# Cross-attention on one Trainium2 core: matmuls regrouped into two-step cycles over three turning pairs of PSUM banks

## What is computed

```python
x = x + _L0_attn_ref(_layernorm(x), gamma, Wq, Wkv, Wo)
x = x + _L0_xattn_ref(_layernorm(x), ctx_2048, mask, Wq, bq, Wk, bk, Wv, bv, Wo, bo, ...)
x = x + _L0_ffn_ref(_layernorm(x), gate_w, gate_b, val_w, val_b, out_w, out_b)
# inside the cross-attention
k = proj(ctx, Wk, bk); v = proj(ctx, Wv, bv)
scores = clip(einsum('bhsd,bhtd->bhst', q, k) / sqrt(16), -50, 50)
scores = where(attend, scores, -10000); scores = clip(scores, -50, 50)
ctx = einsum('bhst,bhtd->bhsd', softmax(scores), v)
delta = ctx @ Wo.T + bo          # then a layernorm, scaled and added
```

## Time and profile before

| | before |
|---|---|
| median of 3 executions | 1391.52 us (1391.16 to 1392.73) |
| the profiled execution | 1393.63 us |
| its span, first to last instruction | 1391.8 us |
| PE busy | 1369.9 us, 98% |
| DVE busy | 996.4 us, 72% |
| ACT busy | 719.7 us, 52% |
| POOL busy | 512.0 us, 37% |
| granted TensorE clock, mean | 0.998 |

### The profile page before, as it was taken

How to read it: one execution, slowest core, us unless ns; L and a number is a source line. 1 busy time by engine, 2 the same in 40 slices (tenths; PEclk the granted TensorE clock), 3 DMA queues, 4 the chain that set the end, 5 groups by cost and what they waited for, 6 DMA issues and landing times.

```text
span 1391.8 us, 55872 instructions
## 1 busy us (share of the span) xinstructions
PE 1369.9 (98%) x25409; PEld 1171.4 (84%) x25409; DVE 996.4 (72%) x1824; ACT 719.7 (52%) x943; POOL 512.0 (37%) x491
## 2 busy tenths in 40 slices
PE   8999999999999999999999999999999999999997
PEld 6788888886888888888888888888888888888884
DVE  5688788785346867777676867677776868677766
ACT  3545454543555555555555555555554555555550
POOL 2656666551324233333323332433333242333310
PEclk9999999999999999999999999999999999999999
DMA  7010001010411211121212121121212112111100
GB/s 193 1 36 1 32 1 32 2 52 1 127 55 47 65 47 50 47 65 32 68 32 78 51 62 50 47 65 32 65 32 80 42 55 65 48 51 47 51 3 8
DMA packets 38957, 66.81 MB, mean 48 GB/s; under 512 B 3749, under 2 KB 36962, under 8 KB 38722
## 3 DMA queue, kind: packets, MB, share of 16 engines
q1 hardware_dynamic: 38722, 63.24, 15.6%
HBM read 61.40 MB, written 1.84 MB: 45 GB/s over the span
## 4 chain that ended last, share of the span: by engine, by line
PE 72%; DVE 2%; issue 0%; POOL 0%; DVEq 0%
PE proj_ps L1479 20%; PE proj_ps L1470 20%; PE score_ps L1497 15%; PE sum_ps L1522 13%; PE side_ps L1557 2%; PE side_ps L1571 1%; PE side_ps L1539 1%; PE side_ps L1564 1%; DVE amax L1357 0%; DVE hidden L1379 0%; DVE sig L1389 0%; DVE hidden L1390 0%; PE side_ps L1546 0%; DVE exps L1279 0%; DVE totals L1301 0%
## 5 line engine op out<-in xcount | busy, mean ns | idle before, releaser
L1231 ACT ACTIVATE exps<-score_ps 125x1792 f32<-125x1792 f32 x192 | 320.4, 1669 | 431.0 <-PE score_ps L1497 431.0
L1279 DVE TENSOR_SCALAR exps<-exps,top 125x896 f32<-125x896 f32 x384 | 287.9, 791 | 21.8 <-ACT exps L1231 17.5
L1497 PE MATMUL score_ps<-spread,keys 32*125 32x112 f32 x6144 | 219.0, 279 | 0.0
L1270 DVE COPY vals<-proj_ps 125x512 f32<-125x512 f32 x192 | 129.5, 687 | 116.7 <-PE proj_ps L1479 114.4
L1522 PEld LDWEIGHTS sum_ps<-exps,vals 125*32 125x32 f32 x12288 | 163.1, 110 | 47.1 <-issue 34.2
L1497 PEld LDWEIGHTS score_ps<-spread,keys 32*125 32x125 f32 x6144 | 184.8, 183 | 15.4 <-issue 0.3
L1522 PE MATMUL sum_ps<-exps,vals 125*32 125x56 f32 x12288 | 191.6, 215 | 0.0
L1159 POOL TENSOR_TENSOR low<-raw_early,high 128x500 fp32r<-128x500 f32 x64 | 84.5, 1322 | 216.8 <-PE proj_ps L1470 215.9
L1159 POOL TENSOR_TENSOR low_early<-raw_early,high_early 128x500 fp32r<-128x500 f32 x62 | 89.4, 1459 | 168.7 <-PE proj_ps L1470 168.7
L1223 ACT ACTIVATE keys<-proj_ps,b_k 128x500 f32<-128x500 f32 x192 | 129.9, 677 | 23.9 <-PE proj_ps L1470 20.4
L331 POOL TENSOR_TENSOR swapped<-swapped,sin 128x448 f32<-128x448 f32 (+1 forms) x69 | 81.0, 1175 | 85.6 <-ACT swapped L615 80.3
(11 more groups left out here) (187 smaller groups left out, 2702.7 us busy)
## 6 DMA issues: line engine op xcount, KB each, us to landing
raw_early<-in_ctxT SPq DMA_DIRECT2D x64, 500.0 KB, 4.2
raw<-in_ctxT SPq DMA_DIRECT2D x32, 500.0 KB, 3.6
w_q<-in_attn_Wq SPq DMA_DIRECT2D x4, 512.0 KB, 9.6
out<-y_out SPq DMA_DIRECT2D x16, 112.0 KB, 2.5
rows<-in_x SPq DMA_DIRECT2D x1, 1344.0 KB, 18.1
raw_early<-in_attn_Wo SPq DMA_DIRECT2D x1, 1024.0 KB, 17.5
raw_early<-in_ffn_gate_wT SPq DMA_DIRECT2D x1, 1024.0 KB, 5.3
raw_early<-in_ffn_val_wT SPq DMA_DIRECT2D x1, 1024.0 KB, 4.9
```

Of the source, the lines that this page charges most:

```text
L1231: nc.scalar.activation(exps[t % 2][:, :, :, :].rearrange("p h r n -> p r h n"), score_ps[0:TILE, :, 0:2 * QW].rearrange("p r (h n) -> p r ...
L1270: nc.vector.tensor_copy(vals[r][:, 2 * q:2 * q + 2, :, 0:HD], proj_ps[q][0:TILE, :].rearrange("p (k h d) -> p k h d", k=2, d=HD))\
L1279: nc.vector.tensor_scalar(tile, tile, LIMIT_LO, top[:, n, at:at + 1], ALU.max, ALU.min)\
L1497: ins = nc.tensor.matmul(score_ps[0:TILE, r, to:to + HE * S], keys[c % 2][32 * r:32 * r + 32, k, (at + half) * TILE:(at + half + 1) * TILE ...
```

## The change

PE's `body` now goes by chunk (`TWINS` = 6 a pair, called a cycle `m` here). With e = 2m and o = 2m + 1 it issues S(e), then A(e-2) and A(e-1) directly behind each other, then S(o), then all four pieces, K and V, of the next chunk. Four runs take the place of six, and tail steps of an odd `t` stand between K and V.

The six banks behind scores and pieces are dealt out anew. `strip_ps` (two banks) takes the second half of every step's scores. Two `pair_ps` of two banks take turns between the first half of the scores and the pieces. S(o) waits for the strip half of the exponential of e and for the copies of the values out of its other two banks; K waits for the whole exponential of e. The exponential of a step is two instructions now, over two banks each, strip half first. A third buffer `exps` lets A lag two steps.

On DVE the limits of e and o stand behind their own exponentials, and both copies of values at the end of the cycle; `divide` and `quantise_hidden` (`AHEAD`, 0 and 10) stand ahead of the limits. On SP each load also waits for the odd scores before it. On POOL the first `power` of a tail stands ahead of the low parts of cycle 1.

```diff
-GATES = (7, 8)
-AFTER = (2, 5)
+TWINS = NT // 2
+SLOTS = 3
@@
-        score_ps = ctx.enter_context(nc.psum_tensor("score_ps", [P, HR, 512], F32))
-        proj_ps = [ctx.enter_context(nc.psum_tensor(f"proj_ps{n}", [P, 512], F32)) for n in range(2)]
+        strip_ps = ctx.enter_context(nc.psum_tensor("strip_ps", [P, HR // 2, 512], F32))
+        pair_ps = [ctx.enter_context(nc.psum_tensor(f"pair_ps{n}", [P, 2, 512], F32)) for n in range(2)]
@@
+        def score_bank(t, r):
+            return pair_ps[(t // 2 + t) % 2][0:TILE, r, :] if r < HR // 2 else strip_ps[0:TILE, r - HR // 2, :]
+        def piece_bank(x, p):
+            return pair_ps[(x + 1) % 2][:, p % 2, :]
@@ SP
                         sp.wait_ge(low_ready, DC * (PC * i + c))
+                        sp.wait_ge(scores_ready, NT * i + 2 * c)
@@ POOL
                 for c in range(PC):
+                    if c == 1 and not first:
+                        power(2 * (i - 1))
@@
                     if c == 1 and not first:
-                        power(2 * (i - 1))
                         power(2 * (i - 1) + 1)
@@ ACT, exp_twin
                 if warm:
-                    act.wait_ge(probs_used, NT * i + t - 1)
-                nc.scalar.activation(exps[t % 2][:, :, :, :].rearrange("p h r n -> p r h n"),
-                                     score_ps[0:TILE, :, 0:2 * QW].rearrange("p r (h n) -> p r h n", h=2),
-                                     ACT.Exp, scale=0.25).then_inc(exps_ready, 1)
+                    act.wait_ge(probs_used, NT * i + t - SLOTS + 1)
+                for at, banks in ((HR // 2, strip_ps), (0, pair_ps[(t // 2 + t) % 2])):
+                    nc.scalar.activation(
+                        exps[t % SLOTS][:, :, at:at + HR // 2, :].rearrange("p h r n -> p r h n"),
+                        banks[0:TILE, :, 0:2 * QW].rearrange("p r (h n) -> p r h n", h=2),
+                        ACT.Exp, scale=0.25).then_inc(exps_ready, 1)
@@ PE, piece
                 elif not cold:
-                    pe.wait_ge(vals_ready, 2 * x + p - 1)
+                    pe.wait_ge(exps_ready, 2 * (2 * x - 1))
@@ PE, scores
-                if warm:
-                    pe.wait_ge(exps_ready, NT * i + t)
+                if t % 2:
+                    pe.wait_ge(exps_ready, 2 * (NT * i + t) - 1)
+                    pe.wait_ge(vals_ready, 2 * (PC * i + c) + 2)
+                elif warm:
+                    pe.wait_ge(exps_ready, 2 * (NT * i + t))
@@ PE, body
+                for m in range(TWINS):
+                    e, o = 2 * m, 2 * m + 1
+                    x, r = PC * i + m + 1, (m + 1) % 2
+                    scores(i, e, not first or e >= 1)
+                    for n in (e - 2, e - 1):
+                        if n >= 0:
+                            add_up(i, n, not first or n >= BN)
+                        elif not first:
+                            add_up(i - 1, NT + n, True)
+                    scores(i, o)
+                    if e in tail:
+                        tail[e]()
+                    if not (last and m == PC - 1):
+                        piece(x, 0, r)
+                        piece(x, 1, r)
+                    if o in tail:
+                        tail[o]()
+                    if not (last and m == PC - 1):
+                        piece(x, 2, r)
+                        piece(x, 3, r)
+                    else:
+                        pe.wait_ge(exps_ready, 2 * (NT * PAIRS - 1))
+                        spare(3)
+                        add_up(i, e, True)
+                    if o == NT - 1 and not first:
+                        tail[NT]()
```

More of the change, by code:

```diff
@@ L1029, in block_b @@
         vals = [sb(f"vals{n}", [TILE, CT, XH, VW]) for n in range(2)]
-        exps = [sb(f"exps{n}", [TILE, 2, HR, QW]) for n in range(2)]
+        exps = [sb(f"exps{n}", [TILE, 2, HR, QW]) for n in range(SLOTS)]
         sums = sb("sums_b", [P, 2, HG // 2, S])
@@ L1222, in keys_out @@
                 act.wait_ge(piece_ready, 4 * x + p + 1)
-                nc.scalar.activation(keys[r][:, p, :], proj_ps[p][:, 0:CHUNK], ACT.Identity,
+                nc.scalar.activation(keys[r][:, p, :], piece_bank(x, p)[:, 0:CHUNK], ACT.Identity,
                                      bias=b_k[:, p:p + 1]).then_inc(keys_ready, 1)
@@ L1240, in body @@
             def body(i, first, last):
[L1241 to L1250, removed]
-                    if not first and t in GATES:
-                        gate_tanh(i - 1, GATES.index(t))
+                for m in range(TWINS):
+                    x = PC * i + m
+                    exp_twin(i, 2 * m, not first or 2 * m >= SLOTS)
+                    if not first and m == 4:
+                        gate_tanh(i - 1, 1)
+                    exp_twin(i, 2 * m + 1, not first or 2 * m + 1 >= SLOTS)
+                    for p in range(DC):
+                        if not (last and m == PC - 1):
+                            keys_out(x + 1, p, (m + 1) % 2)
+                        if not (last and m >= PC - 2):
+                            split_high((m + 2) % 3, 2 * i + (m + 2) // 3 + 1, m % 2, p)
+                    if not first and m == 3:
+                        gate_tanh(i - 1, 0)
             for k in range(DC):
@@ L1417, in body @@
                 tail = {} if first else tail_steps(i - 1, False)
[L1418 to L1419 removed]
+                for m in range(TWINS):
+                    e, o = 2 * m, 2 * m + 1
+                    if e in AHEAD and e in tail:
+                        tail[e]()
                     for k in range(2):
[L1421 to L1425 removed]
+                        limit(i, e, k)
+                    if e == 0 and not first:
                         read_sums(i - 1, 1)
[L1427 removed]
+                    if e == BN:
                         read_sums(i, 0)
[L1429 to L1438 removed]
+                    if e in tail and e not in AHEAD:
+                        tail[e]()
+                    for k in range(2):
+                        limit(i, o, k)
+                    if o in tail:
+                        tail[o]()
+                    if last and o == BN + 3:
+                        divide(i, 0)
+                    for q in range(2) if not (last and m == PC - 1) else ():
+                        values_copy(PC * i + m + 1, q, (m + 1) % 2)
                 if not first:
@@ L1448, in _ @@
             body(LAST, False, True)
-            for half in range(2):
-                limit(LAST, NT - 1, half)
             read_sums(LAST, 1)
@@ L1523, in add_up @@
                                 sum_ps[32 * h:32 * h + VW, g, :], value_and_ones(c % 2, at + half, HJ * g + h),
-                                exps[t % 2][:, half, r, col:col + S],
+                                exps[t % SLOTS][:, half, r, col:col + S],
                                 start=(t % BN == 0 and half == 0 and g == 0),
```

63 lines of the change are left out of this document (19 added, 44 removed).

## The result

| | before | after |
|---|---|---|
| median of 4 executions | 1391.45 us (1391.16 to 1392.73) | 1407.78 us (1404.62 to 1410.89) |
| ratio to before | | 1.0115 (95% interval 1.0087 to 1.0144) |
| the profiled execution | 1393.63 us | 1409.99 us |
| its span | 1391.8 us | 1408.2 us |
| PE busy | 1369.9 us, 98% | 1355.0 us, 96% |

A forecast was written before the change was run, and what follows sets the result against it. PE's own work and its order were taken to bound the kernel; -19.0 - 12.4 + 3.6 + 1.1 = -26.7 us, from the median 1391.5, gave 1364.8 us, range 1358 to 1376.

The forecast's parts named there:

- the second sentence on rows 3: Cross-attention, 360 to 1340 us: PE is no waiting engine, so only its own work or order can shorten the stage.
- V behind K: In the stage, 95 V runs moved from behind S to directly behind K lose 0.20 us each, 19.0 us.
- A behind A and A behind S: In the stage, pairing A runs saves 95 entry costs of 0.13 us, 12.4 us; entry after S taken as 0.13.
- The dearer and the cheaper entry: Rivals on A following S: 0.20 us, adding 6.6 us (0.15 together with dearer tail steps); or down to nothing, 1353 to 1362 (0.08).
- Tail steps between K and V: Odd tail steps moved there from between S and V share no entry cost: 15 pairs x 0.24, 3.6 us given back.
- The start: First cycle of the stage: no A between S(e) and S(o), so PE sits out half an exponential, 1.1 us once.
- The exponential in halves: On ACT: each half takes 0.98 us, ACT grows by 29 us beside PE, costing PE nothing.
- the rival in which ACT bounds the kernel: Half an exponential costs nearly a whole one, V waits for keys every cycle: 1458 us, chance 0.03.
- The edits costed at nothing: Halved exponential, copies, third `exps`, load wait and earlier `power`: none delays PE; the last three have 3 us or more spare.
- The margin of S(o): S(o) waiting for copied values: 2.0 us to spare in a plain cycle, 1.7 in cycle 4, where DVE is fullest.
- both dearer entries together: Rival: A following S costs 0.20 us and tail steps pay an entry after K: 1377 us, chance 0.15 including either alone.
- no gain with a tail that pays nothing: Rival: PE's gaps come with each batch and its waits, so merging runs keeps them: 1392 us, 0.03 for no gain overall.

The follow-up runs named there:

- experiment 11: Changed kernel with satisfied waits as filler on PE, spread over K and V, at most 46 a cycle: 1369.97 us, ratio 0.9849.
- experiment 3: Kernel before, old order, with 128 semaphore increments on PE behind the scores of every even step from the second pair on: 3273.65 us in one execution.
- experiment 9: Changed kernel padded evenly with satisfied waits to 512 PE instructions a cycle, its context loads not waiting for the odd scores: 1380.82 us, ratio 0.9927.
- experiment 1: Changed kernel with semaphore increments strewn behind PE's matmuls of K and V, making every cycle 512 PE instructions: 1469.45 us, ratio 1.0567.
- experiment 10: Changed kernel padded evenly with satisfied waits to 512 PE instructions a cycle, plus 127 more in the first cycle only: 1519.17 us in one execution.
- experiment 4: Changed kernel with one part undone, the context loads no longer waiting for the odd scores: 1440.84 us, ratio 1.0357.

## Why the prediction was wrong

**The step that failed** is the second sentence on rows 3: that nobody holds PE up, "and only what PE itself does, or the way it is ordered, can shorten this stage". It left out what brings PE its instructions. The sum took S, A, K and V to cost the same in any grouping, and no term and no rival priced 384 instructions in 3.85 us. Against the predicted gain, 26.7 + 16.4 = 43 us are missing in the profiled execution; 39.3 of it are the 36 gaps over 0.43 us at the one place of the count (34 of them, 37.6 us, before 1345 us), and the few us left aren't told apart. The rows of before did not show the mechanism, as no block there takes under 5.09 us, but they had the material for the question: the queue with 201 packets, and how many instructions the longest dense place would have.

**V behind K, 19.0 us.** Right. V takes 2.83 us directly behind K throughout, and nothing waits for keys there.

**A behind A and A behind S, 12.4 us.** Right. The two take 1.71 us behind S in every cycle, which is the entry of 0.13 once. The dearer and the cheaper entry are both excluded.

**Tail steps between K and V, 3.6 us given back.** Nearly right. `up` takes 0.43 us there, where 0.46 was said, `turn_hidden` 0.41 as said, `turn_rows` 0.12.

**The start, 1.1 us.** Right: in the chain at the start S(o) stands 1.1 us late, behind ACT's exponential.

**The exponential in halves.** A half takes 0.92 us, not 0.98, and ACT is 13 us busier, not 29. Neither touches PE behind the start, and the rival in which ACT bounds the kernel is excluded: over the whole span it waits 426.1 us for scores, nearly the 431.0 of the kernel before (the 256.3 of the earlier trace rows is for 600 us of it):

```profile
L1244 ACT ACTIVATE exps<-strip_ps 125x896 f32<-125x896 f32 x192 | 176.4, 919 | 426.1 <-PE strip_ps L1513 426.1
```

**The edits costed at nothing.** Here the text was wrong twice. "None is awaited by PE with less than 3 us to spare" does not hold for the power: without its move S(o) waits for DVE's copies by up to 1.0 us, and the move is worth 10.5 us. The margin of S(o) was reckoned for a plain cycle and for cycle 4, and not for cycle 1, where DVE stands still for 2.97 us. And the wait ahead of the loads was taken as a delay that doesn't matter, when it is worth 33 us, about half of it through longer stalls and half with the clock that fell behind them.

**The sum as a whole.** Once the stalls are gone, the order brings what was predicted: experiment 11 is 5.2 us above 1364.8 and inside the range. Of these 5 us the profiled execution shows 1.9 in one wait for DVE, and its pairs at 61.8 to 62.3 us, 0.1 to 0.7 over the shortest lengths added up, nearly all of it in the first cycle of a pair. So the mechanism of the forecast held, and the result has the other sign through one that was not in it. Two slips of the text are small: both dearer entries together come to 1377.4 us, so a range up to 1376 doesn't quite take them in, and no gain with a tail that pays nothing is 1392.6, not 1392.

**What stays open.** No run made the kernel before stall without changing its order: the attempt (experiment 3) used a filler that was too dear. Nor is the limit sharp. Of blocks between 1.8 and 2.7 us in the changed kernel 31 of 48 were followed by a stall; of those between 3.6 and 4.64 us in experiment 11, 2 of 55 (0.4 us); above 4.64 us still 3 of 136 there, 3 of 190 in experiment 9, whose loads come at any time, and 22 of 173 (counted over 0.43 us) in experiment 1 with its increments. The spread goes with the start of the packet. The three blocks of experiment 9 with a stall behind them lasted 5.2 us, but with a load under way their packets started 3.4 to 3.8 us after PE had entered the block. Why a load makes a packet start late, and what sets its start otherwise, no run separates.

## What to carry to other kernels

Count PE's instructions per microsecond, weight loads and waits included, wherever a change groups short matmuls together, and ask whether any 256 of them in a row still last 4 to 5 us, which was enough here but for a few cases. The times of the packets say the same: in the stalls a packet started up to 1.4 us after PE entered a block (2.3 with loads in its way), took 0.9 to 1.7 us, and was of use 1.2 to 1.6 us later. If not, put long matmuls between them or, where the order is worth keeping, pad the long matmuls with satisfied waits so that the borders of the packets fall where they divide the dense run. A wait that ends in "issue" at a different place in each round of a loop, and at equal distances in instructions, points to missing supply and not to a dependency; the times of the instruction queue's packets confirm it or not. A wait on a queue that seems to delay loads for no reason may be what keeps them off such a place: price it by taking it out.

## What the runs showed that I had not expected

- PE's instructions come in packets of 256 (16.4 KB), and each of 94 blocks that PE used up in 1.56 us (experiment 10) was followed by a stall, 0.96 us or more. Every stall there ends 1.1 to 1.6 us after the end of a packet, and that packet started 0.25 to 1.24 us after PE had entered the block that it had just used up.
- Where loads of the context fall on the packets, stalls are longer: 56.0 us instead of 37.6 for 34 of them. The packets take no longer, they start later, 1.39 us after PE enters the block instead of 0.57.
- Longer stalls cost twice where the clock falls behind them: in experiment 4 it was at its lower level for 39 us instead of 7, and ten of the twelve stretches begin within 2 us of a stall of 1.7 us or more. It needn't fall: between 378 and 1483 us experiment 10 has 94 stalls of 0.96 to 2.1 us at full clock.
- Instructions that do nothing can make a kernel faster: 3,823 satisfied waits, 29 us. Spread evenly over K and V, 41 in a cycle cost nothing that shows, 46 cost 0 to 0.6 us by the cycle, and 51 some 0.5 us.
- An increment of a semaphore on PE is another matter: 128 of them took 18.92 us, 0.148 us each.
- The same kernel with the same instructions per cycle took 1377 or 1519 us according to 127 instructions in the stage's first cycle.
